# Ring offsets made once on VectorE, and the query stage's first loads sent behind the last table store

## The chip, the cores and the metric

The kernel runs on one core of one Trainium2 chip. The time is device microseconds of one execution; lower is better. Engines are named as in the profile: PE (TensorE matmul), PEld (its weight load), DVE (VectorE), ACT (ScalarE), POOL (GpSimd) and SP (SyncE). A q behind a name (SPq, POOLq) means the engine's own queue of register, semaphore and DMA-issuing instructions. L1173 is line 1173 of the kernel.

## What is computed

One layer of a graph transformer on 6250 nodes (x: 6250 x 128), 100,000 edges sorted by destination, 8 node types, 8 edge types and 8 heads of 16. W of a node type is a mix of 4 bases.

```python
def _decomp(x, nt, w_comp, w_basis):
    W = (w_comp @ w_basis).reshape(T, x.shape[-1], -1)
    h_all = jnp.einsum('ni,tio->tno', x, W)
    return h_all[nt, jnp.arange(x.shape[0])]
...
k, q, v = (_decomp(...).reshape(n, H, DK) for each)
kt = jnp.einsum('nhi,thij->tnhj', k, relation_att)[edge_type, src]
e = (q[dst] * kt).sum(-1) * relation_pri[edge_type] * scale
m = segment_max(e, dst); ex = exp(e - m[dst])
a = ex / segment_sum(ex, dst)[dst]
vt = jnp.einsum('nhi,thij->tnhj', v, relation_msg)[edge_type, src]
agg = segment_sum(a[..., None] * vt, dst).reshape(n, DH)
out = relu(_decomp(agg, node_type, ...) + x @ loop_weight + bias)
return layernorm(x + out)
```

## The kernel before

It has four stages.

**Table.** For each of the 49 blocks of 128 nodes (7 chunks of 7 blocks) it computes k and v, multiplies them by the relation matrices of the 8 edge types, and stores 1 MB, 8 rows of 256 floats for each node, to `table` in DRAM (SP, L1141, one store a block, four staging slots). Beside that, DVE and POOL build the list of items. The edges are cut into 782 tiles of 128 (`REAL`); an item is a pair of a tile and a node block that it touches. `items()` (L581, on DVE) makes for each item its tile and its block. POOL stores both rows to `item_block` in DRAM and loads them back into one partition each: `iblk` (blocks) and `itile` (tile number plus one).

**Queries.** PE turns x again, multiplies it by the four query bases, and ACT and DVE mix the results into `q_all`. Its first loads are in `queries_in()` on SP: the bases, x chunk 0 and x chunk 1 (two transfers each); ACT issues the later chunks. SP comes to `queries_in()` in the loop over the table's blocks, ahead of the store of block 41 (`QUERIES_AT`).

**Items.** 832 places of items in 26 groups of 32, each group 8 batches of 4. POOL gathers the 128 table rows of each tile by an indirect DMA into a ring of 16 tile slots in SBUF (L1458) and counts in `s_landed` what has landed (L1446). SP copies, for each item, the tile's slot from the ring to `kv`, which holds two groups. That is `bring(n)`, the batch n: it loads four tile numbers into registers (L1152, a TENSOR_LOAD), waits until the kv buffer of two groups ago has been used (`s_weighted`; the wait rides on the next register step, L1170), waits twice for `s_landed`, and issues four copies. Ahead of the third it waits for the copies of batch n - 1 and adds 4 to `s_freed` (L1168); POOL waits for `s_freed` before it overwrites a slot. The ring offset of a copy is worked out in SP's registers:

```python
ring[:, bass.ds(((each[u] - 1) & (RING - 1)) * (2 * D), 2 * D)]
```

DVE multiplies the batch by its queries (`products`, L686) once its four copies are there. PE makes the queries of each edge by a one-hot product (L2012, L2028), ACT makes the one-hot matrices (L1637, L1644) and moves results out of PSUM (L1650), and DVE makes running maxima, weights the values (L794) and adds the sums that PE makes (L2084) into `agg` (L845).

**Last stage.** The seven chunks are normalised, multiplied by the output bases, added to the residual, layer-normed and stored.

Each engine runs its own list of instructions in the order in which the code is written; semaphores order the engines against each other.

Of the kernel before, what the change touches and what calls it, by code (L numbers as in the profile page):

```python
# [5 lines left out]
def graph_transformer_layer(  # L6
# [37 lines left out]
    f32, i32, bf16 = mybir.dt.float32, mybir.dt.int32, mybir.dt.bfloat16  # L44
    ALU, ACT, AX = mybir.AluOpType, mybir.ActivationFunctionType, mybir.AxisListType

    P = 128
    N, D = x.shape
# [27 lines left out]
    IPR = 7  # L76
    ITEMS = P * IPR
# [10 lines left out]
    REAL = -(-E // P)  # L88
    RING = 16
# [8 lines left out]
    item_keys = nc.dram_tensor("item_keys", [3, ITEMS], f32, kind="Internal").ap()  # L98
    base_rows = nc.dram_tensor("base_rows", [NP, D], f32, kind="Internal").ap()
    coef_rows = nc.dram_tensor("coef_rows", [BLOCKS * NB, P], f32, kind="Internal").ap()  # L100
    item_block = nc.dram_tensor("item_block", [2, ITEMS], i32, kind="Internal").ap()

    ctx = ExitStack()
    with ctx:
        def sb(name, shape, dt=f32):
            return ctx.enter_context(nc.sbuf_tensor(name, shape, dt))
# [4 lines left out]
        def sem(name):  # L111
            return ctx.enter_context(nc.semaphore(name))
# [22 lines left out]
        itile = strip[32:33, :].bitcast(i32)  # L135
        iblk = strip[64:65, :].bitcast(i32)
        starts_row = strip[96:97, 0:TILES - 1]
        next_start = starts_row.bitcast(i32)
        band = sb("band", [33, 3 * ITEMS // 2])
        rows8 = band[0:1, 0:3 * H * G]  # L140
        end_run = band[0:1, 3 * H * G:5 * H * G + 2]
        car = band[32:33, :].bitcast(bf16).rearrange("p (k i) -> p k i", k=3)
# [1 line left out]
        kv = sb("kv", [P, 2 * G * 2 * D])  # L144
        ring = sb("ring", [P, RING * 2 * D])
# [48 lines left out]
        h1 = Space(onehot, 2 * G * P)  # L194
# [7 lines left out]
        tcmp = h1.take(TILES)  # L202
        pairs = [h1.take(2 * TILES)]
        fc = h1.take(IPR * 6).rearrange("p (k c) -> p k c", k=6)
        ic = h1.take(IPR * 3).bitcast(i32).rearrange("p (k c) -> p k c", k=3)
        pad_rows = h1.take(P, PADT).bitcast(i32)
        coef_q = Space(onehot, 2 * G * P, at=2 * G * P - BLOCKS * NB).take(BLOCKS * NB)
        assert h1.at <= 2 * G * P - BLOCKS * NB
# [80 lines left out]
        s_item_blocks = sem("s_item_blocks")  # L289
# [33 lines left out]
        s_landed = sem("s_landed")  # L323
# [73 lines left out]
        TILES_AT, STARTS_AT, BIAS_AT, QUERIES_AT = 4, 9, 24, BLOCKS - 8  # L397
# [87 lines left out]
        def _(dve):  # L485
            n = [0]

            def did(ins, name=None):

                n[0] += 1  # L490
                ins.then_inc(s_setup, 1)
                if name:
                    mark[name] = n[0]
                dve.wait_ge(s_setup, n[0])

            v = nc.vector
# [84 lines left out]
            def items():  # L581

                dve.wait_ge(s_column, IPR)
                did(v.tensor_scalar(fc[:, 0, :], fc[:, 0, :], -1.0, None, ALU.add))
                did(v.tensor_copy(ic[:, 0, :], fc[:, 0, :]), "item_tile")
                did(v.tensor_tensor(fc[:, 1, :], fc[:, 1, :], item_no[:, :], ALU.add))
                did(v.tensor_scalar(fc[:, 2, :], fc[:, 1, :], float(BLOCKS - 1), None, ALU.min))
                did(v.tensor_copy(ic[:, 1, :], fc[:, 2, :]))
                did(v.tensor_scalar(fc[:, 2, :], fc[:, 0, :], float(REAL - 1), 1.0, ALU.min, ALU.add))
                did(v.tensor_copy(ic[:, 2, :], fc[:, 2, :]))  # L590
                did(v.tensor_scalar(fc[:, 5, :], fc[:, 1, :], float(P), None, ALU.mult), "item_block")

            def bias_terms():
# [483 lines left out]
        def _(sp):  # L1077
# [28 lines left out]
            for h in range(H):  # L1106
                r = slice(h * DK, (h + 1) * DK)
                c = h * DK % RW
# [14 lines left out]
            def queries_in():  # L1123

                sp.wait_ge(s_stage0, STAGE0)
                sp.dma_start(Bq.rearrange("p (b d) -> p b d", b=NB),
                             basis_q.rearrange("b (i o) -> i b o", o=D)).then_inc(s_q_bases, 16)
                x_again(0, 0)
                x_again(1, 1)

            for n in range(BLOCKS):
                ch = n // CB + 2
                if n % CB == 2 and ch < CHUNKS:
                    x_chunk(ch)
                    types_chunk(ch)
                if n == QUERIES_AT:
                    queries_in()
                if n in SPLIT:
                    sp.wait_ge(s_table_split, SPLIT.index(n) * 2 + 2)
                sp.wait_ge(s_table_copied, copied(n))  # L1140
                sp.dma_start(table[n * P * T:(n + 1) * P * T, :].rearrange("(p t) f -> p t f", t=T),  # L1141
                             stage[:, n % SLOTS, :, :]).then_inc(s_table_stored[n % SLOTS], 16)

            for g in range(2):
                seg3 = seg[:, g * (IH * P + 1):g * (IH * P + 1) + IH * P].rearrange("p (i e) -> p i e", i=IH)
                for i in range(IH):
                    sp.dma_start(seg3[:, i, :], item_bias[g * G + i * IL:g * G + i * IL + IL, :]
                                 .rearrange("(a l) e -> a l e", a=1).broadcast_to([H, IL, P]))\
                        .then_inc(s_segments[g], 16)

            def tiles_of(i, count):
                return nc.values_load_multi_w_load_instructions(  # L1152
                    itile[0:1, i:i + count], engines=(sp.engine,), min_val=1, max_val=REAL,
                    skip_runtime_bounds_check_because="clamped when written")[1]

            sp.wait_ge(s_item_blocks, 48)

            def bring(n):

                g, b = n // NBATCH, n % NBATCH  # L1160
                par = g % 2
                each = tiles_of(4 * n, 4)
                after(sp, s_weighted, g - 2, NBATCH, b + 1)
                for u in range(4):
                    if u == 2 and n > 0:
                        sp.wait_ge(s_gathered[(n - 1) // NBATCH % 2][(n - 1) % NBATCH],
                                   (n - 1) // (2 * NBATCH) * 64 + 64)
                        sp.sem_inc(s_freed, 4)  # L1168
                    if u % 2 == 0:
                        sp.wait_ge(s_landed, each[u + 1] & 1023)  # L1170
                        hold_apart(sp)
                    o = (par * G + b * 4 + u) * 2 * D
                    sp.dma_start(kv[:, o:o + 2 * D],  # L1173
                                 ring[:, bass.ds(((each[u] - 1) & (RING - 1)) * (2 * D), 2 * D)])\
                        .then_inc(s_gathered[par][b], 16)

            for n in range(12):
# [112 lines left out]
        def _(pool):  # L1290
# [41 lines left out]
            n = [0]  # L1332
# [43 lines left out]
                    out=irows[:, k, :], out_offset=None, in_=tile_rows,  # L1376
                    in_offset=bass.IndirectOffsetOnAxis(ap=ic[:, 0, k:k + 1], axis=0)).then_inc(s_item_rows, 16)
            pool.wait_ge(s_setup, mark["item_block"])
            pool.dma_start(item_block.rearrange("a (p c) -> p a c", c=IPR), ic[:, 1:3, :]).then_inc(s_item_blocks, 16)
            pool.wait_ge(s_item_blocks, 16)  # L1380
            pool.dma_start(iblk[:, :], item_block[0:1, :]).then_inc(s_item_blocks, 16)
            pool.dma_start(itile[:, :], item_block[1:2, :]).then_inc(s_item_blocks, 16)

            pool.wait_ge(s_item_rows, 16 * IPR)
            did(g_.tensor_copy(lanes, irows))
# [62 lines left out]
            for t in range(REAL):  # L1448
                if t >= AHEAD:
                    landed(t - AHEAD)  # L1450
                if t >= RING and t % 2 == 0:
                    (done,) = nc.values_load_multi_w_load_instructions(
                        next_start[0:1, t + 1 - RING:t + 2 - RING], engines=(pool.engine,), min_val=1,
                        max_val=GROUPS * G, skip_runtime_bounds_check_because="counted from tiles")[1]
                    pool.wait_ge(s_freed, done & 1023)
                    hold_apart(pool)
                o = t % RING * 2 * D
# [389 lines left out]
        def _(pe):  # L1847
# [149 lines left out]
            query_products(CHUNKS - 1, 0)  # L1997


            pe.wait_ge(s_item_blocks, 48)  # L2000
            L = IH * P
            HG = H * G

# [264 lines left out]
```

## Time and profile before

| | |
|---|---|
| times of three runs | 1735.99, 1752.89, 1755.89 us; median 1752.89 |
| the profiled execution | 1759.41 us, its span 1757.2 us |
| mean granted PE clock in it | 0.783 |
| instructions in the span | 31429 |

The span runs from the first to the last instruction of the profiled execution; the rest of its time lies around it. All rows below are of that one execution. "Busy" leaves out register, semaphore and DMA-issuing instructions, so SP has no busy time; what SP does is seen in the chain and in the lines with SPq.

### The profile page before, as it was taken

The numbers are of one execution on the slowest core, as the hardware profiler recorded it, in microseconds if no ns is written. First come the engines' busy times: TensorE is split into PE (matmuls) and PEld (weight loads), VectorE is DVE, ScalarE is ACT, GpSimd is POOL, SyncE is SP. The second block draws the span as 40 slices with busy tenths as digits, with TensorE's granted clock in tenths as the row PEclk, the third lists the DMA queues.
The fourth block names the chain that finished last, engine by engine and source line by source line (L and its number), as shares of the span: only waits on it lengthen the run. The fifth ranks groups of instructions, "written<-read, shape, count | busy, mean of one in ns | idle before, by whom it ended". The sixth has DMA issues, their size and how long they took to land.

```text
span 1757.2 us, 31429 instructions
## 1 busy us (share of the span) xinstructions
PE 1160.7 (66%) x6730; PEld 962.9 (55%) x6730; DVE 986.6 (56%) x2832; ACT 785.6 (45%) x2217; POOL 881.5 (50%) x915
## 2 busy tenths in 40 slices
PE   8989875657556565566566655566565666656698
PEld 5445434656545554455455554565455565545587
DVE  7877463555445555445555554455554566545677
ACT  4667454444434434443344343443444354434324
POOL 2775354555555554545454545455545554545233
PEclk9999997777677767876777667766777687777699
DMA  8878754555555555545455555555555555555675
GB/s 261 323 289 316 284 172 140 157 148 158 152 159 153 157 151 151 149 141 151 150 163 148 158 152 154 148 160 164 151 162 154 154 168 148 155 150 162 187 242 194
DMA packets 225149, 309.08 MB, mean 176 GB/s; under 512 B 32423, under 2 KB 191119, under 8 KB 217781
## 3 DMA queue, kind: packets, MB, share of 16 engines
q1 hardware_dynamic: 159996, 188.75, 30.6%
q0 software_dynamic: 38880, 106.25, 23.4%
q10 hardware_dynamic: 26088, 12.08, 2.4%
q8 instruction: 61, 1.00, 0.2%
q14 instruction: 124, 1.01, 0.2%
HBM read 139.52 MB, written 58.78 MB: 113 GB/s over the span
## 4 chain that ended last, share of the span: by engine, by line
SPq 34%; issue 31%; PE 12%; DVE 9%; another core or an unknown queue 7%; DMA 2%; DVEq 2%; ACT 1%; POOL 1%; POOLq 0%; ACTq 0%
SPq L1173 27%; PE pb L1900 4%; SPq L1152 2%; PE pb L1923 2%; DVE agg L845 2%; SPq L481 2%; SPq L1170 2%; DVEq L814 2%; DMA kv<-ring 2%; PE pb L2084 1%; SPq L1168 1%; PE pb L2190 1%; PE pb L2028 1%; DVE kv L541 1%
## 5 line engine op out<-in xcount | busy, mean ns | idle before, releaser
L1458 POOL DMA_INDIRECT ring<-table,rows_idx x782 | 745.8, 954 | 736.6 <-SPq L1168 452.5
L2084 PE MATMUL pb<-work,onehot 128*128 128x136 f32 x1664 | 367.5, 358 | 214.1 <-DVE agg L845 152.8
L845 DVE TENSOR_TENSOR agg<-agg,pb 128x136 f32 x832 | 241.8, 291 | 459.9 <-remote 291.8
L2084 PEld LDWEIGHTS pb<-work,onehot 128*128 128x128 f32 x1664 | 307.0, 254 | 242.0 <-issue 210.9
L1650 ACT ACTIVATE work<-pb 128x512 f32<-128x512 f32 x208 | 124.0, 596 | 549.6 <-remote 376.2
L2028 PE MATMUL pb<-q_all,work 128*128 x1664 | 301.0, 340 | 1.3 <-issue 0.8
L2028 PEld LDWEIGHTS pb<-q_all,work 128*128 128x128 f32 x1664 | 280.6, 253 | 7.6 <-issue 4.9
L1637 ACT ACTIVATE work<-lane,neg_lane 128x128 f32<-128x128 f32 x800 | 253.3, 390 | 0.6
L2012 PE MATMUL pb<-ident,onehot 128*128 128x128 f32 x832 | 174.5, 347 | 115.6 <-issue 60.2
L2012 PEld LDWEIGHTS pb<-ident,onehot 128*128 128x128 f32 x832 | 125.4, 180 | 136.0 <-issue 71.3
L686 DVE TENSOR_TENSOR kv<-kv,pb 128x512 f32<-128x512 f32 x208 | 141.5, 680 | 96.6 <-issue 41.7
L1670 ACT ACTIVATE pb<-work 128x32 f32<-128x32 f32 x200 | 42.9, 215 | 228.7 <-DVE work L779 129.0
L696 DVE TENSOR_REDUCE work<-kv 128x32 f32<-128x512 f32 x208 | 141.4, 680 | 0.4
L794 DVE TENSOR_TENSOR work<-kv,pb 128x512 f32<-128x512 f32 x200 | 136.2, 681 | 5.7 <-ACT work L1671 3.8
L1644 ACT ACTIVATE onehot<-work 128x512 f32<-128x512 f32 x200 | 125.9, 630 | 6.3
L1557 ACT ACTIVATE kv<-pb 128x512 f32<-128x512 f32 x190 | 98.5, 602 | 43.1 <-PE pb L1923 38.8
L1900 PE MATMUL pb<-work,kv 128*128 128x512 f32 x196 | 108.1, 634 | 8.3 <-DVE kv L541 6.9
L541 DVE SCALAR_TENSOR_TENSOR kv<-pb,onehot,kv 128x128 f32<-128x128 f32 x294 | 80.4, 341 | 0.4 <-PE pb L1900 0.2
L2057 PE MATMUL pb<-ones,end_out 1*128 1x1 f32 x208 | 41.8, 318 | 53.3 <-DVE end_out L758 19.6
L2048 PE MATMUL pb<-ident,work 128*1 128x128 f32 x104 | 20.4, 332 | 82.9 <-DVE work L731 55.0
L2057 PEld LDWEIGHTS pb<-ones,end_out 1*128 1x128 f32 x208 | 39.6, 280 | 61.7 <-DVE end_out L758 21.5
L1923 PE MATMUL pb<-onehot,kv 32*128 32x256 f32 x784 | 60.1, 401 | 1.5 <-issue 0.9
(239 smaller groups left out, 1237.2 us busy)
## 6 DMA issues: line engine op xcount, KB each, us to landing
kv<-ring SPq DMA_DIRECT2D x832, 128.0 KB
table<-kv SPq DMA_DIRECT2D x49, 1024.0 KB, 5.2
ring<-table,rows_idx POOLq DMA_INDIRECT x782
kv<-base_rows SPq DMA_DIRECT2D x7, 448.0 KB, 7.6
kv<-in_x_dram SPq DMA_DIRECT2D x8, 384.0 KB, 5.8
seg<-item_bias ACTq DMA_DIRECT2D x48, 64.0 KB
base_rows<-pair ACTq DMA_DIRECT2D x24, 128.0 KB
onehot<-coef_rows SPq DMA_DIRECT2D x3, 1024.0 KB, 5.5
```

Of the source, the lines that this page charges most:

```text
L686: v.tensor_tensor(rows_of(par, b)[:, :, 0:D], rows_of(par, b)[:, :, 0:D], PB[2 + b % 2][:, :].rearrange("p (u d) -> p u d", u=4), ALU.mult)\
L696: v.tensor_reduce(sc[:, :, l0:l0 + 4].rearrange("p h l -> p l h"), rows_of(par, b)[:, :, 0:D].rearrange("p u (h k) -> p u h k", h=H), AX.X ...
L794: v.tensor_tensor(w[:, :, 0:D].rearrange("p u (h k) -> p u h k", h=H), rows.rearrange("p u (h k) -> p u h k", h=H), weights_of(b).unsqueez ...
L845: v.tensor_tensor(a, a, PB[banks[i // 2 % len(banks)]][:, (i % 2) * 256:(i % 2) * 256 + W], ALU.add).then_inc(s_added, 1)
L1173: sp.dma_start(kv[:, o:o + 2 * D], ring[:, bass.ds(((each[u] - 1) & (RING - 1)) * (2 * D), 2 * D)])\
L1458: pool.indirect_dma_start(out=ring[:, o:o + 2 * D], out_offset=None, in_=table, in_offset=bass.IndirectOffsetOnAxis(ap=rows_idx[:, t:t + 1 ...
L1637: square = a_.activation(sq[:, u, :], lane[:, :], ACT.Square, bias=neg_lane[:, bass.ds(g * G + b * 4 + u, 1)])
L1644: a_.activation(onehot[:, o:o + 4 * P], sq[:, :, :].rearrange("p u e -> p (u e)"), ACT.Relu, bias=1.0, scale=-1.0).then_inc(s_one_hot, 1)
L1900: t_.matmul(PB[2 + half][:, :], xT[:, c * P:(c + 1) * P], Bkv[:, 2 * half:2 * half + 2, :, :].rearrange("p b k d -> p (b k d)"), start=Tru ...
L2012: mm = t_.transpose(PB[0][:, u * P:(u + 1) * P], onehot[:, o:o + P], ident[:, :])
L2028: mm = t_.matmul(PB[2 + b % 2][:, u * D:(u + 1) * D], spread[:, b % 2, u, :], q_all[:, bass.ds(blks[u] * D, D)], start=True, stop=True)
L2084: mm = t_.matmul(PB[banks[k % len(banks)]][:, u * 256:u * 256 + W], onehot[:, o:o + P], wv[:, b % WR, h * 2 + u, :], start=True, stop=True)
```

## The change

`items()` makes a third row for each item, the offset of its tile's slot in the ring: the tile number modulo 16, times 256. POOL stores three rows instead of two and loads the third into a new partition of `band`, `iplace`. `bring` loads four offsets from there in one TENSOR_LOAD, and of the tile numbers only the two that it waits for. `queries_in()` moves behind the loop over the table's blocks.

```diff
-    item_block = nc.dram_tensor("item_block", [2, ITEMS], i32, kind="Internal").ap()
+    item_block = nc.dram_tensor("item_block", [3, ITEMS], i32, kind="Internal").ap()
...
+        iplace = band[64:65, 0:ITEMS].bitcast(i32)
...
                 did(v.tensor_copy(ic[:, 2, :], fc[:, 2, :]))
+                did(v.tensor_scalar(fc[:, 2, :], fc[:, 2, :], -1.0, None, ALU.add))
+                did(v.tensor_copy(ic[:, 3, :], fc[:, 2, :]))
+                did(v.tensor_scalar(ic[:, 3, :], ic[:, 3, :], RING.bit_length() - 1, None,
+                                    ALU.logical_shift_right))
+                did(v.tensor_copy(fc[:, 3, :], ic[:, 3, :]))
+                did(v.scalar_tensor_tensor(fc[:, 2, :], fc[:, 3, :], float(-RING), fc[:, 2, :],
+                                           ALU.mult, ALU.add))
+                did(v.tensor_scalar(fc[:, 2, :], fc[:, 2, :], float(2 * D), None, ALU.mult))
+                did(v.tensor_copy(ic[:, 3, :], fc[:, 2, :]))
                 did(v.tensor_scalar(fc[:, 5, :], fc[:, 1, :], float(P), None, ALU.mult), "item_block")
...
-                if n == QUERIES_AT:
-                    queries_in()
                 if n in SPLIT:
                     sp.wait_ge(s_table_split, SPLIT.index(n) * 2 + 2)
...
+            queries_in()
             for g in range(2):
...
-            def tiles_of(i, count):
+            def places_of(i, count):
                 return nc.values_load_multi_w_load_instructions(
-                    itile[0:1, i:i + count], engines=(sp.engine,), min_val=1, max_val=REAL,
+                    iplace[0:1, i:i + count], engines=(sp.engine,), min_val=0, max_val=(RING - 1) * 2 * D,
...
+            def landings_of(i):
+                return nc.values_load_multi_w_load_instructions(
+                    itile[0:1, i + 1:i + 4:2], engines=(sp.engine,), min_val=1, max_val=REAL,
...
-            sp.wait_ge(s_item_blocks, 48)
+            sp.wait_ge(s_item_blocks, 64)
...
-                each = tiles_of(4 * n, 4)
+                places = places_of(4 * n, 4)
+                landings = landings_of(4 * n)
...
-                        sp.wait_ge(s_landed, each[u + 1] & 1023)
+                        sp.wait_ge(s_landed, landings[u // 2] & 1023)
                         hold_apart(sp)
                     o = (par * G + b * 4 + u) * 2 * D
-                    sp.dma_start(kv[:, o:o + 2 * D],
-                                 ring[:, bass.ds(((each[u] - 1) & (RING - 1)) * (2 * D), 2 * D)])\
+                    sp.dma_start(kv[:, o:o + 2 * D], ring[:, bass.ds(places[u], 2 * D)])\
                         .then_inc(s_gathered[par][b], 16)
...
-            pool.dma_start(item_block.rearrange("a (p c) -> p a c", c=IPR), ic[:, 1:3, :]).then_inc(s_item_blocks, 16)
+            pool.dma_start(item_block.rearrange("a (p c) -> p a c", c=IPR), ic[:, 1:4, :]).then_inc(s_item_blocks, 16)
...
+            pool.dma_start(iplace[:, :], item_block[2:3, :]).then_inc(s_item_blocks, 16)
...
-            pe.wait_ge(s_item_blocks, 48)
+            pe.wait_ge(s_item_blocks, 64)
```

On SP, from the table's last stores to the seg loads that come ahead of batch 0, before (table is the DRAM table, onehot holds the query bases and x here, x8 is a count of equal rows):

```order
L1141 DMA table<-kv 128x2048 x11
L1126 DMA onehot<-in_L_gnn_w_basis_q_dram 128x4x128
L1117 DMA onehot<-in_x_dram 128x6x128
L1120 DMA onehot<-in_x_dram 128x128
L1141 DMA table<-kv 128x2048 x8
L1147 DMA seg<-item_bias 128x1x128 x4
```

and now, at the same place:

```order
L1149 DMA table<-kv 128x2048 x19
L1136 DMA onehot<-in_L_gnn_w_basis_q_dram 128x4x128
L1127 DMA onehot<-in_x_dram 128x6x128
L1130 DMA onehot<-in_x_dram 128x128
L1156 DMA seg<-item_bias 128x1x128 x4
```

The bases and both chunks of x (the second chunk's two rows repeat the first's) have moved past the last eight stores.

On SP, the first half of a batch of four copies, before (strip holds the tile numbers; the REGISTER_ALU at L1170 masks the number to wait for, those at L1173 and the ISA row make the offset and the address):

```order
L1152 TENSOR_LOAD strip
L1170 REGISTER_ALU
L1173 REGISTER_ALU x2
L1173 ISA
L1173 DMA kv<-ring 128x256
```

and now (band holds the ready offsets; L1188 is the copy):

```order
L1161 TENSOR_LOAD band
L1166 TENSOR_LOAD strip
L1185 REGISTER_ALU
L1188 ISA
L1188 DMA kv<-ring 128x256
```

Two register steps are gone ahead of each copy, four copies a batch, and one TENSOR_LOAD a batch has come; three instructions a batch that only wait or count are not in these rows and stay.

## Rows read from the trace of the kernel before

**Rows 1.** The page: busy time (share of the span), and the chain by engine and line.
```profile
PE 1160.7 (66%) x6730; PEld 962.9 (55%) x6730; DVE 986.6 (56%) x2832; ACT 785.6 (45%) x2217; POOL 881.5 (50%) x915
...
SPq 34%; issue 31%; PE 12%; DVE 9%; another core or an unknown queue 7%; DMA 2%; DVEq 2%; ACT 1%; POOL 1%; POOLq 0%; ACTq 0%
SPq L1173 27%; PE pb L1900 4%; SPq L1152 2%; PE pb L1923 2%; DVE agg L845 2%; SPq L481 2%; SPq L1170 2%; DVEq L814 2%; DMA kv<-ring 2%; PE pb L2084 1%; SPq L1168 1%; PE pb L2190 1%; PE pb L2028 1%; DVE kv L541 1%
```

**Rows 2.** The chain by line, from 380 to 740 us, then from 1080 to 1340 us.
```profile
by line: SPq L1173 43.2%; issue 42.3%; SPq L1152 4.5%; SPq L481 3.1%; SPq L1168 2.5%; SPq L1170 2.3%; DMA kv<-ring 1.9%; POOL ring L1458 0.2%; POOLq L1452 0.1%; POOLq L481 0.0%; POOLq L1455 0.0%; POOLq L1446 0.0%
...
by line: another core or an unknown queue 37.0%; issue 16.7%; DVE agg L845 6.4%; DVEq L814 5.8%; PE pb L2084 5.2%; PE pb L2028 4.1%; PE pb L2012 3.5%; ACT work L1637 2.4%; DVE work L794 1.7%; DVE work L770 1.3%; DVE band L746 1.3%; DVE band
```

**Rows 3.** SP's own waits: line, releaser, us in total, times, longest.
```profile
SPq L1168 <- DMA kv<-ring: 3.6, 7, 1.1
```

**Rows 4.** Line L1168, who waited for it: us in total, times.
```profile
  POOL ring L1458: 472.8, 128
```

**Rows 5.** Line L1173, 331.8 to 1126 us: ns min/median/max, first and last start.
```profile
L1173 SPq DMA_DIRECT2D kv<-ring x448: 2/486/1189, 331.9 to 1124.8; - x150
```

**Rows 6.** Pieces of the chain, 879 to 896 us: start, us, what.
```profile
879.76 0.30 SPq L1152
...
886.24 0.72 SPq L1173
...
891.22 0.30 SPq L1152
...
893.44 0.04 SPq L1173
...
893.51 0.04 SPq L1173
...
894.98 0.30 SPq L1152
```

**Rows 7.** Windows: us, busy us (instructions) by engine; clock, DMA share, GB/s last.
```profile
880.00:890.00 10.00, 6.10 (x39) 5.69 (x39) 3.10 (x9) 3.18 (x10) 6.64 (x7) 0.84 0.62 169
890.60:895.40 4.80, 2.67 (x19) 2.30 (x20) 4.18 (x11) 4.08 (x13) 1.04 (x2) 0.97 0.33 111
740.00:1080.00 340.00, 206.00 (x1116) 186.32 (x1116) 175.07 (x478) 142.45 (x423) 171.72 (x180) 0.73 0.51 152
```

**Rows 8.** Line L686, 347.2 to 1140 and 1140 to 1512.4 us; idle before it (us, times).
```profile
L686 DVE TENSOR_TENSOR kv<-kv,pb x112: 662/680/690, 347.3 to 1127.6; 128x512 f32<-128x512 f32 x112
...
  issue: 31.4, 19
  DMA kv<-ring: 23.0, 14
...
L686 DVE TENSOR_TENSOR kv<-kv,pb x56: 661/680/689, 1140.1 to 1507.7; 128x512 f32<-128x512 f32 x56
...
  issue: 1.5, 2
  DMA kv<-ring: 1.5, 1
```

**Rows 9.** Timeline of PE, then POOL, where queries and gathers begin: start, us; [idle before].
```profile
193.00 0.63 PE L1969 MATMUL pb<-ident,onehot 128*128 128x128 f32 x4 [1.28 <-ACT kv L1557]
...
199.15 1.06 POOL L1458 DMA_INDIRECT ring<-table,rows_idx  x1 [38.80 <-DMA table<-kv]
```

**Rows 10.** Lines L1126 and L1120 (queries); L1085 (same 64 KB part, table stage), its landing.
```profile
L1126 SPq DMA_DIRECT2D onehot<-in_L_gnn_w_basis_q_dram x1: 2127/2127/2127, 169.5 to 169.5; - x1
...
L1120 SPq DMA_DIRECT2D onehot<-in_x_dram x2: 561/972/1382, 172.3 to 173.4; - x2
...
DMA to landing us min/median/max: 3.6/6.4/7.0
```

**Rows 11.** Timeline of DVE at the start of items().
```profile
89.46 0.17 DVE L584 TENSOR_SCALAR onehot<-onehot 128x7 f32<-128x7 f32 x1
89.67 0.17 DVE L585 CAST onehot<-onehot 128x7 int32<-128x7 f32 x1
```

More of the change, by code:

```diff
@@ L138, in graph_transformer_layer @@
         next_start = starts_row.bitcast(i32)
-        band = sb("band", [33, 3 * ITEMS // 2])
+        band = sb("band", [65, 3 * ITEMS // 2])
+        iplace = band[64:65, 0:ITEMS].bitcast(i32)
         rows8 = band[0:1, 0:3 * H * G]
@@ L204, in graph_transformer_layer @@
         fc = h1.take(IPR * 6).rearrange("p (k c) -> p k c", k=6)
-        ic = h1.take(IPR * 3).bitcast(i32).rearrange("p (k c) -> p k c", k=3)
+        ic = h1.take(IPR * 4).bitcast(i32).rearrange("p (k c) -> p k c", k=4)
         pad_rows = h1.take(P, PADT).bitcast(i32)
@@ L1149, in _ @@
                         .then_inc(s_segments[g], 16)
-            def tiles_of(i, count):
+            def places_of(i, count):
                 return nc.values_load_multi_w_load_instructions(
-                    itile[0:1, i:i + count], engines=(sp.engine,), min_val=1, max_val=REAL,
+                    iplace[0:1, i:i + count], engines=(sp.engine,), min_val=0, max_val=(RING - 1) * 2 * D,
+                    skip_runtime_bounds_check_because="a remainder by the ring's size when written")[1]
+            def landings_of(i):
+                return nc.values_load_multi_w_load_instructions(
+                    itile[0:1, i + 1:i + 4:2], engines=(sp.engine,), min_val=1, max_val=REAL,
                     skip_runtime_bounds_check_because="clamped when written")[1]
-            sp.wait_ge(s_item_blocks, 48)
+            sp.wait_ge(s_item_blocks, 64)
             def bring(n):
```

## The prediction

> **What bounds the kernel now.** I read the page first [rows 1]: no engine is busy for more than two thirds of the span, and 34% of the chain that ended last lies on SyncE's own instructions (SPq), most of it on L1173, the line that computes a ring offset and issues one copy ring -> kv. The reader is to see that a queue which computes nothing leads the chain. Next the chain by stretches [rows 2]: from 380 to 740 us it hardly leaves SyncE (two more stretches, 740 to 1080 and 1340 to 1560 us, read the same), while from 1080 to 1340 us it lies on DVE, PE and ACT. So two limits are close together. Third, SyncE's own waits: after the table the longest entry on the copies is 3.6 us at L1168 [rows 3], and L1170, where it would wait for a freed kv buffer, is not in that list at all; POOL in turn is idle for 472.8 us until L1168 has freed ring slots [rows 4]. SyncE is always at work, and both sides wait for it.
>
> How fast is it? Between 331.9 and 1124.8 us it started 448 copies [rows 5], 447 intervals: 7.10 us for a batch of four. The pieces of the chain show two gears [rows 6]. From the TENSOR_LOAD at 891.22 to the next at 894.98 a batch takes 3.76 us. The batch before, 879.76 to 891.22, takes 11.46 us: the same 22 instructions, but the register step at 886.24 takes 0.72 us where the one at 893.44 takes 0.04. The windows show what else happens [rows 7]: in the slow stretch of 10.0 us POOL issues 7 gathers and is busy for 66%, and DVE falls to 31%; in the fast one POOL is at 22% and DVE at 87%. No row names the cause; that slow SyncE, slow DVE and gathers go together is shown. A mean of 7.10 between 3.76 and 11.46 means that 43% of a batch's steps are done in the slow gear: 4.97 us of slow and 2.13 us of fast time per batch.
>
> Then the customer. DVE's products (L686) need the batch's copies [rows 8]. The 112 that begin at 347.3 us come every 7.08 us (the next window's first is at 1140.1), and DVE is idle before them for 31.4 + 23.0 = 54.4 us. In the next 56, from 1140.1 to 1507.7 us, the idle time is 3.0 us and the pace 367.6/55 = 6.68 us. So 6.68 us is what the engines need when the data is there.
>
> **The change part by part.** *Ring offsets.* Per batch, eight register steps go (two at each of four copies), the TENSOR_LOAD of places comes, and the old one loads two values instead of four: 22 instructions become 15. In the fast gear a register step costs 0.07 us (893.44 to the next at 893.51) and a load 0.30 us [rows 6]: 3.76 - 8 x 0.07 + 0.30 = 3.50 us. In the slow gear an instruction costs 11.46/22 = 0.52 us, so 15 cost 7.8 us. With the same 4.97 us of slow time a batch gets 0.64 of itself done there; the other 0.36 takes 1.27 us: 6.24 us per batch. Bounds: if the slow gear is paid by the copy and not by the step, only the fast part is shortened, 4.97 + 0.566 x 3.50 = 6.95 us; if all goes by the count, 7.10 x 15/22 = 4.8 us. I take 6.24, since the slow step of [rows 6] is a register step, of just the kind that goes.
>
> At 6.24 us SyncE is quicker than the engines' 6.68 us, and the stall goes to them: what is late next is the batch's own work on DVE, PE and ACT, and SyncE begins to wait for kv buffers. The gain is what the engines were starved of: (7.08 - 6.68) x 112 = **-45 us** (by the idle times 54.4 us, less the 0.05 us per batch that stays, 48). Before 347 us the engines are behind (the query stage runs while SyncE already copies), and the windows from 1140 us on are not starved, so nothing is counted there. At 6.95 us the gain is only 0.13 x 112 = 15 us.
>
> The wait for the places (64 instead of 48 on s_item_blocks) costs nothing: the third load is one more of POOL's in front of the idle time of 38.8 us that POOL has before its first gather [rows 9], and SyncE and PE come to that wait after the table. Without that cover it would be the landing of one small load, once.
>
> *Seven more DVE steps in items().* The eight there stand one by one at 0.21 us [rows 11], in a stage in which DVE has little idle time: 7 x 0.21 = **+1.5 us** (0 if PE is late there; no more in any case).
>
> *The query loads.* At table row 41 five transfers leave the queue from 169.5 us on [rows 10], ahead of store 41. POOL's wait for the stores ends with the last one, seven rows later, which goes out when its copy is done; so nothing is won there: 0 (a bound below nothing: some 5 us, the span of the five issues, had their delay gone through to the last store). In their new place they start behind the last store, which waits for the table's last copy. That copy is also what releases PE's first turn at 193.00 us now [rows 9], so they start then. The second part of the first chunk was issued 2.8 us after the bases (169.5, 172.3), and such a part lands 3.6 to 7.0 us after its issue [rows 10]: ready at 199.4 to 202.8 us. I take 201, **+8 us** (bounds 6.4 and 9.8), since it has a full store ahead of it in its queue. Work that would hide it: none on PE, ACT or DVE; POOL's first gather at 199.15 us waits for the stores alone and stays. The seg loads and the first copy move back by the five issues on SyncE; the first copy waits for POOL's gathers there anyway, and compute reaches group 0 tens of us later.
>
> *Sum against the profiled execution:* 1759.4 - 45 + 8 + 1.5 = 1724 us. The median of the runs is 6.5 us below that execution: **1717 us**, 2.0% below 1752.9. Some 2% is what a measurement of this kernel can tell from no change, so the forecast lies on that line.
>
> *A rule against the change.* A copy's issue takes 0.49 us (median) [rows 5], four of them 1.9 of the 7.1 us of a batch, and the DMA share is no more than 0.33 just where SyncE is fast [rows 7], so the transfers themselves have room. The Trainium skill, "DMA: Bandwidth & Descriptors", Issuing engines are not separate DMA queues, says that all issuers share the same 16 DMA engines and that the time to initiate a DMA is usually small beside the DMA. By that rule a shorter issue would win nothing, and the sum would be 1753 + 9.5 = 1762 us; the trace does not agree with it here. I leave that case 0.05, inside rival 1.
>
> **Rivals.** 1. *SyncE, or the transfer, stays the bound.* If the slow gear is paid per copy the pace is 6.95 us: 1753 - 15 + 9.5 = 1748 us; with nothing won, 1762. For it: the copies and their semaphore waits stay, and one more load comes in. Against: [rows 6].
>
> 2. *The engines pay for denser gathers (slower).* A quicker SyncE reaches its next L1168 inside a slow stretch, POOL gets four more tiles without a pause, and stretches of 7 gathers in 10.0 us [rows 7] become the rule. 782 gathers in 208 batches then make 3.76 x 10.0/7 = 5.4 us of slow time per batch instead of 4.97. DVE has 3.65 us of work per batch (175.07 us in 340 us [rows 7], at 7.08 us a batch); at 31% it gets 1.7 us of it done in the slow time, and the other 1.95 us take 2.2 us at 87%: 7.6 us per batch, +0.5 x 168 = 84, with the 9.5 us 1847 us; half of it 1805. It decides once POOL's pauses for L1168 (472.8 us in 128 [rows 4]) shrink by more than the engines' idle time does. For it: DVE's 31%. Against: today's shares already contain starved time, and the waits for kv buffers will hold SyncE back.
>
> 3. *The engines get faster as well*, because with a filled kv buffer they also work where they now wait for a slow stretch to end: SyncE's 6.24 us for all 168 batches, (7.08 - 6.24) x 112 + (6.68 - 6.24) x 56 = 119 us, 1753 - 119 + 9.5 = 1644 us; as a middle 1680. For it: 6.68 was measured with SyncE only little ahead. Against: from 1080 to 1340 us the chain lies on the engines themselves [rows 2].
>
> That the change doesn't do what it says has no chance of its own: the order of the instructions shows the register steps gone and the transfers moved.
>
> **How the numbers follow.** Forecast 0.50, its own range 1700 to 1735 (a gain of 27 to 62 us), half of it beyond 2%. Rival 1: 0.23, within 2%. Rival 2: 0.13, mostly slower. Rival 3: 0.14, faster. Faster: 0.25 + 0.14 = 0.39; slower 0.11; within 2% 0.25 + 0.23 + 0.02 = 0.50. The range leaves out most of rival 2 and the far end of rival 3: 1672 to 1764 us.
>
> **What would show it.** Right: SyncE's batch near 6.2 us where it doesn't wait, waits of tens of us at the s_weighted wait, idle time before the products nearly gone, their pace at 6.7 us, PE's first query turn at about 201 us. Wrong: products slower than 7.0 us with SyncE waiting (rival 2); SyncE without waits and at 7 us (rival 1); products under 6.4 us (rival 3); or a first product that comes more than 10 us later than now.

## The result and the profile after

| | before | changed |
|---|---|---|
| median, us | 1751.91 (4 runs) | 1840.16 (1833.41 to 1846.67, 4 runs) |
| ratio to before | 1 | 1.052, 95% interval 1.044 to 1.061: slower |
| profiled execution, span | 1757.2 | 1831.6 |

The forecast was 1717 us, the range 1672 to 1764. Medians here and below are of all runs of a kernel and ratios of its fast runs alone, so they can differ: of e11's four runs two are slow, over 1.5% above its fastest, and of e13's ten six (medians without them 1631 and 1733 us).

The page of the changed kernel, busy time and chain, beside [rows 1]:

```profile
PE 1159.0 (63%) x6730; PEld 963.7 (53%) x6730; DVE 986.3 (54%) x2839; ACT 784.6 (43%) x2217; POOL 877.8 (48%) x916
...
PE 29%; another core or an unknown queue 26%; DVE 18%; issue 15%; DVEq 7%; ACT 4%; DMA 1%; SPq 0%; ACTq 0%
```

SyncE has left the chain (34% before, 0% now), as forecast, and the busy times are the same to 0.5%. But in its place stands "another core or an unknown queue", 26% against 7%: time in which an engine waits and the view names no releaser. SyncE's own waits and POOL's for line 1183, where ring slots are freed, beside [rows 3, 4]:

```profile
SPq L1185 <- DVE work L804: 111.2, 20, 8.1
...
SPq L1183 <- DMA kv<-ring: 0.2, 1, 0.2
```

```profile
  POOL ring L1473: 523.6, 108
```

SyncE now waits for kv buffers (the s_weighted wait, us in total, times, longest), so it is ahead of the engines. POOL waits less often for free slots (108 times, not 128) and longer each time. The products of the same 112 batches as in [rows 8]:

```profile
L696 DVE TENSOR_TENSOR kv<-kv,pb x112: 662/680/682, 372.0 to 1196.7; 128x512 f32<-128x512 f32 x112
```

111 intervals in 824.7 us, 7.43 us a batch, where before it was 780.3/111 = 7.03. No idle time before them is listed any more, so the data is there, and the pace is worse. Where the time is, seen in one run of eight gathers, first by POOL's timeline, then by windows (us, then busy time and instructions of PE, PEld, DVE, ACT, POOL; granted clock, DMA share and GB/s last):

```profile
885.77 0.94 POOL L1473 DMA_INDIRECT ring<-table,rows_idx  x1 [4.11 <-SPq L1183]
887.01 0.95 POOL L1473 DMA_INDIRECT ring<-table,rows_idx  x1 [0.30 <-issue]
...
894.52 0.95 POOL L1473 DMA_INDIRECT ring<-table,rows_idx  x1 [0.30 <-issue]
900.28 0.94 POOL L1473 DMA_INDIRECT ring<-table,rows_idx  x1 [4.81 <-SPq L1183]
```

```profile
885.80:891.50 5.70, 5.39 (x44) 4.75 (x43) 3.50 (x9) 3.73 (x13) 4.48 (x5) 1.00 0.59 178
891.50:897.60 6.10, 0.00 (x0) 0.00 (x0) 0.00 (x0) 0.00 (x0) 3.06 (x4) 0.85 0.47 144
897.60:900.20 2.60, 1.31 (x5) 1.02 (x6) 2.57 (x7) 2.51 (x7) 0.00 (x0) 0.50 0.19 64
900.20:906.00 5.80, 5.80 (x38) 5.43 (x38) 3.35 (x9) 3.85 (x12) 4.47 (x5) 0.80 0.66 199
906.00:912.10 6.10, 0.02 (x1) 0.00 (x0) 0.00 (x0) 0.00 (x0) 3.10 (x4) 0.78 0.50 151
```

The run lasts from 885.77 to 895.47 us. DVE's last instruction ends 3.7 us after its start, ACT's 4.2 and PE's 5.7; then all three stand still for 6.1 us, until 2.1 us after POOL's last gather. The next run repeats it. The DMA share is half or less meanwhile, so on the mean the 16 DMA engines have room. I call such a stretch a standstill below: over 0.3 us without an instruction of PE, DVE or ACT under way.

What each engine waits for is seen in the last and the next instructions of the three (DVE, ACT, PE):

```profile
889.22 0.29 DVE L855 TENSOR_TENSOR agg<-agg,pb 128x136 f32 x1
897.63 0.29 DVE L855 TENSOR_TENSOR agg<-agg,pb 128x136 f32 x1 [8.12 <-remote]
...
897.66 0.60 ACT L1665 ACTIVATE work<-pb 128x512 f32<-128x512 f32 x1 [7.64 <-remote]
...
889.98 0.63 PE L2099 MATMUL pb<-work,onehot 128*128 128x136 f32 x4
890.44 1.05 PE L2043 MATMUL pb<-q_all,work 128*128 x8
898.88 1.24 PE L2099 MATMUL pb<-work,onehot 128*128 128x136 f32 x4 [7.38 <-DVE agg L855]
```

DVE's next sum waits for `s_item_sums`, which only PE's L2099 raises, and ACT's next move for two counts that only PE's L2027 and L2043 raise. PE's records of all three end by 891.49 us, yet the waits end 6 us later; the view shows this as "remote". PE itself waits for DVE's sum. So the engines wait for PE's results. This is the rule: the changed kernel has 76 standstills of over 1 us between the first products of groups 2 and 24, and 70 of them end with a count that PE raises, recorded a median 6.0 us behind the end of the matmul (61 of 65 in the kernel before, 4.7 us). Whether PE's matmuls hang or only their signals is not shown, since the trace models the ends of matmuls.

A standstill also costs more than its length. PE has no instruction from 891.49 us on, and its granted clock falls to 0.50, the lower of its two levels (1.2 and 2.4 GHz); it is there for all of the third window, and the four matmuls of L2099 take 1.24 us in place of 0.63.

At the start PE's first query turn is 10.9 us later than in [rows 9] (8 forecast), and it waits for the x that was moved:

```profile
203.90 1.08 PE L1984 MATMUL pb<-ident,onehot 128*128 128x128 f32 x4 [8.97 <-DMA onehot<-in_x_dram]
```

By group 2 the changed kernel is 372.0 - 347.3 = 24.7 us behind, by group 24 (products at 1642.4, before at 1566.5 us) 75.9 us; the spans differ by 74.4. The 24.7 us are not taken apart below: the offsets alone (e1) lose 23.2 us by group 2, the moved loads alone (e2) 17.4.

### The profile page after: what moved, and what is told of

Same layout as the page of the kernel before. It is cut to its first block, busy times and chain, and to the rows that moved or that the text cites. A ratio compares the mean times of both kernels' runs of the same rounds, so it can differ in the third digit from the quotient of the medians.

```text
span 1831.6 us, 29981 instructions
## 1 busy us (share of the span) xinstructions
PE 1159.0 (63%) x6730; PEld 963.7 (53%) x6730; DVE 986.3 (54%) x2839; ACT 784.6 (43%) x2217; POOL 877.8 (48%) x916
## 4 chain that ended last, share of the span: by engine, by line
PE 29%; another core or an unknown queue 26%; DVE 18%; issue 15%; DVEq 7%; ACT 4%; DMA 1%; SPq 0%; ACTq 0%
PE pb L2099 7%; DVEq L824 6%; DVE agg L855 5%; PE pb L1915 5%; PE pb L2043 4%; PE pb L1938 3%; PE pb L2027 2%; PE pb L1995 2%; DVE work L804 1%; ACT work L1652 1%; PE pb L2072 1%; DVE kv L696 1%; DVEq L855 1%; DVE band L756 1%
## 5 line engine op out<-in xcount | busy, mean ns | idle before, releaser
L1473 POOL DMA_INDIRECT ring<-table,rows_idx x782 | 742.1, 949 | 793.4 <-SPq L1183 523.6
L2099 PE MATMUL pb<-work,onehot 128*128 128x136 f32 x1664 | 373.2, 362 | 269.1 <-DVE agg L855 161.8
L2099 PEld LDWEIGHTS pb<-work,onehot 128*128 128x128 f32 x1664 | 314.4, 260 | 296.8 <-issue 262.0
L2043 PE MATMUL pb<-q_all,work 128*128 x1664 | 296.9, 337 | 5.1 <-issue 4.6
L2043 PEld LDWEIGHTS pb<-q_all,work 128*128 128x128 f32 x1664 | 277.4, 250 | 8.1 <-issue 6.0
L2027 PE MATMUL pb<-ident,onehot 128*128 128x128 f32 x832 | 171.5, 342 | 84.3 <-issue 37.2
L2027 PEld LDWEIGHTS pb<-ident,onehot 128*128 128x128 f32 x832 | 121.4, 176 | 108.5 <-issue 59.6
L2063 PEld LDWEIGHTS pb<-ident,work 128*1 128x1 f32 x104 | 8.6, 98 | 114.2 <-DVE work L741 98.9
```

Of the source, the lines that this page charges most:

```text
L1473: pool.indirect_dma_start(out=ring[:, o:o + 2 * D], out_offset=None, in_=table, in_offset=bass.IndirectOffsetOnAxis(ap=rows_idx[:, t:t + 1 ...
L2027: mm = t_.transpose(PB[0][:, u * P:(u + 1) * P], onehot[:, o:o + P], ident[:, :])
L2043: mm = t_.matmul(PB[2 + b % 2][:, u * D:(u + 1) * D], spread[:, b % 2, u, :], q_all[:, bass.ds(blks[u] * D, D)], start=True, stop=True)
L2099: mm = t_.matmul(PB[banks[k % len(banks)]][:, u * 256:u * 256 + W], onehot[:, o:o + P], wv[:, b % WR, h * 2 + u, :], start=True, stop=True)
```

## The experiments

Theory A: a run of eight gathers makes the engines stand still, and a SyncE that frees slots inside a run makes such runs. Rivals: B the moved query loads, C the longer loads on SyncE, D the engines' own order, E SyncE's lead, F POOL's mean rate.

All runs but e5 and e6 in one table. "Pace", "runs" and "standstill" are worked out from each trace from the first product of group 2 to that of group 24 (176 batches): a run is a row of gathers whose starts lie under 1.6 us apart, counted by length; the standstill (as above) is given per batch, and "rest" is the pace without it. The profiled executions lie within 1% of their kernel's median, but for e7 (1843 us, 2.2% above, so its row does not show the gain of its median) and e13 (1719 us, 2.1% below). "places" are the ready offsets.

| kernel | median us | ratio to before (95%) | pace | runs of 4 / of 8 | standstill | rest |
|---|---|---|---|---|---|---|
| before | 1755 | 1 | 6.93 | 52 / 41 | 1.12 | 5.80 |
| changed | 1840 | 1.044 to 1.061 | 7.22 | 18 / 56 | 1.64 | 5.58 |
| e1 places only | 1847 | 1.046 to 1.064 | 7.38 | 19 / 56 | 1.93 | 5.44 |
| e2 loads moved only | 1755 | 0.998 to 1.007 | 6.88 | 71 / 31 | 1.20 | 5.69 |
| e3 e1, steps kept | 1776 | 1.005 to 1.022 | 7.07 | 111 / 14 | 0.75 | 6.32 |
| e4 e1, short lead | 1810 | 1.026 to 1.046 | 7.01 | 64 / 36 | 1.38 | 5.63 |
| e7 e1, 3 in flight | 1803 | 1.018 to 1.031 | 7.33 | 88 / 0 | 1.59 | 5.74 |
| e8 e1, drains | 1919 | 1.085 to 1.096 | 7.81 | 158 / 0 | 1.21 | 6.60 |
| e9 e1, pause each 4 | 1611 | 0.913 to 0.932 | 6.08 | 153 / 0 | 0.56 | 5.52 |
| e11 before, pause each 4 | 1648 | 0.922 to 0.945 | 6.45 | 126 / 0 | 0.73 | 5.72 |
| e12 e1, pause each 8 | 1756 | 0.996 to 1.004 | 6.98 | 23 / 37 | 1.53 | 5.46 |
| e15 e1, half pause each 4 | 1848 | 1.039 to 1.059 | 7.42 | 119 / 0 | 1.70 | 5.72 |
| e14 e1, half pause each 2 | 1848 | 1.037 to 1.054 | 7.31 | 0 / 0 | 1.13 | 6.18 |
| e10 e1, one load of six | 1809 | 1.029 to 1.048 | 7.22 | 27 / 51 | 1.69 | 5.53 |
| e13 e10, pause each 4 | 1756 | 0.987 to 0.999 | 6.71 | 138 / 0 | 0.97 | 5.73 |
| e16 changed, pause each 4 | 1694 | 0.953 to 0.968 | 6.55 | 138 / 0 | 0.83 | 5.72 |
| e17 e3, pause each 4 | 1706 | 0.964 to 0.976 | 6.71 | 116 / 0 | 0.71 | 6.00 |

**e1 and e2: the two parts apart.**

```diff
(e1, against the changed kernel; e2 makes the opposite edit in the kernel before)
+                if n == QUERIES_AT:
+                    queries_in()
...
-            queries_in()
```

> Ready offsets alone; the query loads are back ahead of store 41. Theory A (the offsets cost the time: SyncE is no longer the bound, POOL gathers eight tiles in a row and the engines pay): the query loads account for the 18.6 us by which the first product came late, the rest stays: 1815 to 1828 us, pace of the products from group 2 on about 58 us a group as in the changed kernel. Theory B (the move of the query loads shifts the rhythm of everything behind it and is the larger part): 1752 to 1780 us, pace about 55.5 us a group.

> The moved query loads alone, ring offsets worked out in registers as before. By the prediction's term, +8 us: 1761 us. By the first product of the changed kernel (18.6 us later): 1768 to 1775 us. Theory B: 1800 us or more.

The offsets carry all of it (e1 1.055), the moved loads nothing that can be measured (1.003), though PE's first query turn in e2 comes at 201.32 us, just where the forecast put it. B is out.

```profile
201.32 1.09 PE L1968 MATMUL pb<-ident,onehot 128*128 128x128 f32 x4 [9.62 <-DMA onehot<-in_x_dram]
```

**e3 and e4: SyncE made slow again, or held back.**

```diff
(e3, against e1: the loaded row holds tile numbers)
-ring[:, bass.ds(places[u], 2 * D)]
+ring[:, bass.ds(((places[u] - 1) & (RING - 1)) * (2 * D), 2 * D)]
(e4, against e1)
+                if n > 3:
+                    sp.wait_ge(s_products, n - 2)
```

> As e1, but the row that is loaded holds tile numbers and the eight register steps of a batch stay: before plus one load of two values a batch (and the seven steps on VectorE). Theory A (a quicker SyncE lets the engines down): with the steps back SyncE is slower again than the engines, POOL mostly stops after four tiles, 1753 plus at most 112 x 0.3 us for the load, 1755 to 1790 us. Rival C (the second load is what costs, each load waits for something on its way to the core's memory): as e1 or slower, 1815 to 1850 us, with loads of 0.6 to 0.9 us.

> As e1, but batch n is not brought before the products of batch n - 3 are made (one more wait of SyncE, on a semaphore that is there). Theory A in the form that SyncE's lead of five batches is what lets POOL run eight gathers at a time: POOL is released batch by batch, 1740 to 1770 us. Rival C or an engine cost that has nothing to do with the lead: 1815 us or more.

e3 does all of e1's work and eight register steps a batch more, and is 71 us faster. Its chain lies on SyncE again and has none of the unexplained time (e3, then e1):

```profile
SPq 54%; issue 30%; PE 9%; DVE 5%; DVEq 1%; DMA 0%; ACT 0%; POOL 0%; POOLq 0%; another core or an unknown queue 0%; ACTq 0%
```

```profile
another core or an unknown queue 30%; PE 26%; DVE 18%; issue 14%; DVEq 8%; ACT 3%; DMA 0%; SPq 0%; ACTq 0%
```

So removing the steps is what hurts: 71 of the 92 us. e4 gives back 37 of 92 us and still has 36 runs of eight; it missed its 1740 to 1770.

**e5 and e6: no gathers.** Every tile from the 17th on is reported as landed without a transfer.

```diff
(both; the indirect DMA and the wait for its semaphore stand under this condition)
+                if t < RING:
```

> As e1, but POOL gathers only the first 16 tiles; every later tile is reported as landed without a transfer (the copies bring old rows, so the values are not the reference's; all other work stays). Theory A (what is slow are the stretches with gathers: in e1 the engines stand still for 7.96 us inside one run of eight gathers): without them the engines' chain of a batch takes some 5 us, 208 batches give 1300 to 1500 us. Rival D (the engines' own order needs 6.7 us a batch and more, gathers or not): 1650 us or more.

> The kernel before with the same work left out (gathers of tiles 16 and on, reported as landed at once). Theory A: SyncE then runs in its fast gear, 3.76 us a batch, ahead of the engines, so register steps or not make no difference: within 1% of e5. Rival D or a cost of the loads themselves: e5 and e6 differ by 3% or more, as e1 and the kernel before do.

1273 and 1222 us: the gathers cost some 530 us in the kernel before and 574 in e1. Without gathers the products come every 4.50 us in e5 and every 4.26 us in e6 (groups 2 to 24, as in the table), so the engines' own order needs far less than 6.7 us a batch; D is out. PE's busy time for the same groups is 602 us in e6, at a mean granted clock of 0.85, and 736 us in the changed kernel, at 0.73. In the piece of 7.96 us of e1 that e5's expectation calls a standstill, PE was still busy for 2.0 us and ACT for 0.4. That e5 and e6 differ by 4% was not expected by A: here C is seen. The chain of e5, then of e6:

```profile
SPq 50%; PE 18%; issue 13%; DVE 9%; DMA 4%; ACT 3%; DVEq 1%; another core or an unknown queue 1%; POOLq 1%; ACTq 0%
```

```profile
PE 37%; DVE 25%; ACT 19%; issue 12%; DVEq 4%; ACTq 1%; DMA 1%; another core or an unknown queue 0%; SPq 0%
```

SyncE's loads by line (ns min/median/max), two in e5, then the one of e6:

```profile
L1162 SPq TENSOR_LOAD <-band x208: 485/818/1135, 198.2 to 1169.9; - x104
...
L1167 SPq TENSOR_LOAD <-strip x208: 625/630/822, 199.0 to 1170.5; - x104
```

```profile
L1152 SPq TENSOR_LOAD <-strip x208: 293/302/943, 196.1 to 1121.4; - x104
```

The two loads take 0.82 + 0.63 us in place of 0.30. On the chain of e5 one batch goes from load to load in 4.42 us:

```profile
700.78 0.83 SPq L1162
...
705.20 0.82 SPq L1162
```

In the fast gear the changed SyncE is thus slower than before (3.76 us [rows 6]); what it can gain it gains in the slow gear, where a register step takes 0.72 us [rows 6], that is, only while gathers run. Just there it frees the next slots.

**e7 and e8: two ways to thin the gathers that failed.**

```diff
(e7, against e1)
-    AHEAD = 7
+    AHEAD = 3
(e8, against e1)
-                if t >= AHEAD:
-                    landed(t - AHEAD)
+                while told < (t if t % 4 == 0 else t - AHEAD + 1):
+                    landed(told)
+                    told += 1
```

> As e1, but POOL waits for the gather three tiles back instead of seven before it issues the next. If the standstill comes from gathers that pile up unfinished (POOL issues one in 1.26 us), it shrinks with fewer in flight: 1700 to 1800 us. If it belongs to any time in which gathers are under way, runs only get longer: 1840 us or more.

> As e1, but before every fourth gather POOL waits until all earlier ones have landed, so that no run is longer than four; SyncE's lead stays. Theory A with the length of a run as the cause (about 4 us of work go on in a run before the engines stop, whatever its length): 1740 to 1800 us. If only the number of gathers counts: as e1, 1840 us or more, since the drains make POOL slower.

e7 gives 45 us back by its median. Its runs are cut in the count, but by short waits, and a run of four stands still for 1.64 us. In e8 each drain lasts some 3.4 us and the gathers become the bound, so it tells nothing about A:

```profile
issue 30%; DMA 28%; POOL 18%; PE 9%; SPq 7%; POOLq 4%; DVE 4%; DVEq 0%; ACT 0%; ACTq 0%
```

**e9, e11 and e12: a pause on POOL.**

```diff
(e9 against e1, e11 against the kernel before)
+                if t >= RING and t % 4 == 3:
+                    pool.wait_ge(s_paused, (t - RING) // 4)
+                    g_.memset(band[96:128, :], 0.0).then_inc(s_paused, 1)
(e12: two such memsets where t % 8 == 7)
```

> As e1, with a pause of some 1.5 to 2 us on POOL after every fourth gather (a memset of an unused strip), so that a run of eight is cut into two of four; SyncE, its loads and its lead stay. Theory A (in a run of four all engines together stand still for about 1 us, in one of eight for 4 to 5 us): nearly all 56 runs of eight go, 56 x 2 us or more come back, 1720 to 1790 us. Rival E (the lead or the loads of SyncE are what costs, the runs only go with it): as e1, 1835 to 1860 us.

> The kernel before with the same pause on POOL after every fourth gather. Theory A: its 42 runs of eight are cut too, where the engines stand still for 3.4 us each, against 0.85 us in a run of four; as far as SyncE, which stays slow, lets it: 1700 to 1750 us. Rival E: POOL only gets later, 1755 to 1800 us.

> As e9, but two memsets after every eighth gather instead of one after every fourth: the same work on POOL, the same mean rate, runs of eight left whole. Theory A (the length of a run decides): the standstill of some 4 us a run stays, 1740 us or more. Theory F (POOL's mean rate, or the memset as such, is what helps): 1595 to 1640 us, as e9.

POOL's timeline in e9; the pause is 1.24 us, with the issue 1.40 between two gathers:

```profile
825.43 0.95 POOL L1475 DMA_INDIRECT ring<-table,rows_idx  x1 [0.30 <-issue]
826.38 1.24 POOL L1481 MEMSET band<- 32x1344 f32 x1
827.78 0.96 POOL L1475 DMA_INDIRECT ring<-table,rows_idx  x1 [0.16 <-issue]
```

Extra work on POOL makes e1 236 us faster and the kernel before 108 us, both more than A's ranges. With one memset fewer (190), in pairs after every eighth gather, runs of eight stay and the time is 1756: 145 us of e9's gain hang on where the pauses stand. F, the mean rate, is left with at most the other 91. The loads and the lead (C and E) are in e9 as in e1, so they are not the main cost; e10 below and e4 put 38 and 37 us on them. The page of e9 shows the gain where A puts it: the wait for slots is no longer POOL's main one, and the unexplained share of the chain is down to 16%, while e12 has 27%.

```profile
PE 38%; DVE 18%; issue 16%; another core or an unknown queue 16%; ACT 7%; DVEq 4%; DMA 0%; SPq 0%; ACTq 0%
...
L1475 POOL DMA_INDIRECT ring<-table,rows_idx x782 | 748.5, 957 | 320.6 <-issue 209.8
```

**e14 and e15: shorter pauses.**

```diff
(e15, against e9; e14 does it after every second gather)
-                    g_.memset(band[96:128, :], 0.0).then_inc(s_paused, 1)
+                    g_.memset(band[96:128, 0:672], 0.0).then_inc(s_paused, 1)
```

> As e9, but a memset of half the length after every second gather. Theory A: runs of two, less standstill still (0.3 to 0.5 us a run), if the pause is long enough to end a run; POOL somewhat slower by the fixed part of a memset: 1580 to 1640 us. Theory F: as e9 by its rate. If the shorter pause does not end a run: 1750 us or more.

> As e9 with a memset of half the length after every fourth gather. Theory A: the pause need only let the queued gathers drain; if 0.7 us is enough, POOL is quicker and 1580 to 1611 us; if it is too short for that, part of the standstill is back: 1650 to 1800 us.

A memset of 0.68 us does nothing (1848, as e1), though POOL does more work than in e1; the standstill of a run of four is 1.75 us in e15, 0.60 in e9. In e15 the starts on either side of the memset lie 1.8 us apart, just enough to end a run as counted here; in e9 it is 2.35 us. So e15 and e7 show that the count of a run is not the cause by itself: the gap has to be long enough. How long was tried at these points alone. e14 has shorter standstills and a longer rest; why the rest grew is not settled.

**e10, e13, e16 and e17: does a quicker SyncE pay, once there is a pause?**

```diff
(e10, against e1; the landings are stored behind the places, six numbers a batch; e13 adds e9's pause)
-                places = places_of(4 * n, 4)
-                landings = landings_of(4 * n)
+                places = places_of(6 * n, 6)
+                landings = places[4:6]
(e16: the changed kernel with e9's pause; e17: e3 with it)
```

> As e1, but the four places and the two landings of a batch stand side by side and come in one load of six values, where e1 has two loads of 0.80 and 0.63 us. Theory A: the engines, not SyncE, set e1's pace, and a still quicker SyncE frees slots earlier: 1840 to 1870 us. Rival C (the longer loads are the cost): the load back at 0.3 to 0.5 us, the time back at 1750 us or below.

> The one load of six of e10 together with the pause of e9. Theory A: with the runs cut, the quicker SyncE does no harm; e9 is held by the engines and by POOL (four gathers and a pause, 6.3 us), so 1590 to 1630 us, no clear difference to e9. If SyncE still holds e9: up to 3% faster.

> The whole changed kernel (offsets and moved query loads) with the pause of e9. If e9's gain comes from what it says, standstills cut whatever the phase, the moved loads add nothing to speak of (e2): 1600 to 1640 us. If e9 hit a favourable rhythm of SyncE, POOL and engines that a shift of a few us breaks (as e13 suggests, 145 us slower than e9 with the same pause): 1680 to 1770 us.

> The kernel of e3 (two loads and all register steps, the slowest SyncE) with the pause. If SyncE's pace is a term of its own once runs are short, the order is e9 (1611), the kernel before with the pause (1648), this one: 1665 to 1720 us. If SyncE's pace has no such order: at or under 1648 us, or over 1750 us.

The load of six takes 1.06 us, less than the two together, and e10 is 38 us faster than e1, not slower: it met neither theory's range. With the pause, the order is e9 1611, before 1648, e16 1694, e17 1706, e13 1756. It does not follow SyncE's pace: e13 has the quickest SyncE and is last, and e16 differs from e9 by the moved loads alone, which cost nothing without the pause. The pause helped in all five (by 53 to 236 us); how much depends on the rhythm in which SyncE, POOL and the engines fall in, and what sets that is not settled.

A's ranges were met by e3, e12 and, by its second branch, e14. The times of e1, e4, e7 (by 3 us), e8, e13 and e15 are above them, those of e5, e9, e10 and e11 below, and e6 was not within 1% of e5: A names the place of the loss, but not its size. In e16 the branch in which the rhythm decides was met, in e17 the one in which SyncE's pace does.

## Why the prediction was wrong

**The step that failed** is "So 6.68 us is what the engines need when the data is there", and with it the -45 us. It took the engines' pace as their own. It is a result of when the gathers run: with the data there the changed kernel needs 7.22 us a batch, and 4.26 us are enough without gathers (e6). In the table the rest is 5.4 to 5.8 us in all kernels but e3, e17 (SyncE's chain), e8 (the gathers') and e14, with places or without, and the standstill beside it moves between 0.56 and 1.93 us. The change took 0.22 us of rest a batch away, which I read as the starving that I meant to win, and added 0.52 us of standstill: 0.3 x 176 = 51 us (with unrounded paces 7.218 and 6.927), which is what groups 2 to 23 lost. The rest is itself 1.3 us above e6's 4.26 us; PE's busy time is 0.8 us a batch longer at the lower clock, which may be a part of that, and the remainder is not settled.

**The load was mis-sized too.** "3.76 - 8 x 0.07 + 0.30 = 3.50 us" took the second load at the price of the first; the two take 1.43 us in the changed kernel (medians, beside 0.30 [rows 6]):

```profile
L1161 SPq TENSOR_LOAD <-band x208: 3/804/1402, 204.1 to 1732.8; - x104
```

```profile
L1166 SPq TENSOR_LOAD <-strip x208: 3/628/1402, 205.0 to 1733.3; - x104
```

So the fast gear became slower. It did not set the time, since SyncE is off the chain; it does where there are no gathers (e5).

**Rival 2** came closest, with the right place and the right start: slots freed inside a slow stretch, runs of eight as the rule (41 to 56). Its price, 1847 us, was near by luck. It counted more slow time with DVE at 31%, while packets of gathers are under way for no more time than before (3.49 us a batch, before 3.65), and the engines do not slow down in a long run but stop (the windows above). Its sum was off too: the 56 batches that had run at 6.68 us would lose 0.9 us each by it, not 0.5, which gives 1872 us. Its condition, POOL's pauses shrinking in total, did not come true (472.8 to 523.6 us); fewer and longer pauses was the sign. The objection that "the waits for kv buffers will hold SyncE back" failed: it waits for 111.2 us, but in 20 lumps of up to 8.1, and runs of eight are made between them.

**Right were** SyncE leaving the chain, the waits at s_weighted, the idle time gone, PE's first turn (201 forecast, 201.32 in e2, 203.90 here), and that the seven steps on VectorE are next to nothing (DVE's busy time is 986.3 us, before 986.6; they were not tried alone). The +8 us of the query loads did not reach the end: e2 is 1755 us (0.998 to 1.007). The first product came 18.6 us late, which the prediction had named as a sign of being wrong; in e1, with the loads in their old place, it still comes 15 us late (281.3 us), so most of that is the offsets as well.

The rule of the Trainium skill that was weighed ("DMA: Bandwidth & Descriptors", Issuing engines are not separate DMA queues) would have given 1762 us. That a shorter issue wins nothing was so, but not for its reason: the DMA share in the two standstills above is 0.47 and 0.50.

## What to carry to other kernels

A queue that leads the chain may also be the brake that keeps other queues apart. Before it is made quicker, look at what it releases and whether that lands inside another burst; the idle engines' stretches in a burst (windows in which several engines read 0.00 at once) show the price, and an average pace doesn't. A pause in the burst was worth 3 to 13% here where 2% was forecast from a quicker SyncE, but its length (1.24 us, not 0.68) and place had to be found by trial.

## What the hardware showed

- In a run of eight indirect DMAs by GpSimd, one in 1.25 us, PE, DVE and ACT come to a common stop: the standstills of over 1 us begin a median 6.6 us after the first gather in the changed kernel and 7.8 in the kernel before, and end 2.0 us after the last. A run of four cost 0.7 us of standstill in the kernel before, one of eight 3.2, in the changed kernel 4.2. Without gathers there are no standstills (e6: none over 0.3 us in 176 batches).
- What DVE and ACT wait for in them is PE: 70 of 76 end with a count of PE's that comes a median 6.0 us after the record of its matmul. Which resource is held is not shown; only 3 instead of 7 gathers in flight (e7) did not help much.
- The clock granted to PE fell to 0.50 in such a standstill, and the same four matmuls then took 1.24 us instead of 0.63.
- A load into SyncE's registers took 0.30 us for four values in the kernel before, and in the kernels with places 0.63 for two (every second value), 0.80 to 0.82 for four from another tile, 1.06 for six from there.
